# fp32 local attention: clamp on GpSimd, q's length in the score pass instead of the exponentials, squares first in each bank, another order of the steps

## What is computed

```python
h = shift_token(x)
q, k, v = jnp.split(h @ wqkv, 3, axis=-1)       # 128 -> 3 x 512
q = l2norm(q) * qs
k = l2norm(k) * ksc
q, k = rotary_xpos(q, k)                        # q * cos * scale + rotate_half(q) * sin * scale
...
sim = jnp.einsum('bhwid,bhwjd->bhwij', bq, bk)  # q times 8
sim = jnp.where(mask, -jnp.finfo(sim.dtype).max, sim)
attn = jax.nn.softmax(sim, axis=-1)
out = jnp.einsum('bhwij,bhwjd->bhwid', attn, bv)
x = x + out @ wo
```

## Time and profile before

| | us |
|---|---|
| three timed runs | 495.89, 494.99, 490.20 |
| their median | 494.99 |
| the profiled execution | 490.59 |
| its span in the trace | 488.8 |

### The profile page before, as it was taken

The page is one execution under the profiler, slowest core; times in us unless marked ns, Lnnn a source line. Parts: engine busy times, 40 slices in busy tenths (PEclk is TensorE's granted clock), DMA queues, the critical chain, the costliest instruction groups (busy, mean ns, idle before and its releaser), DMA issues.

```text
span 488.8 us, 8090 instructions
## 1 busy us (share of the span) xinstructions
PE 403.8 (83%) x2504; PEld 261.2 (53%) x2504; DVE 366.4 (75%) x1404; ACT 322.5 (66%) x986; POOL 199.5 (41%) x197
## 2 busy tenths in 40 slices
PE   0688858889989998978689678998999899877895
PEld 0466644556655665666434236665666566654342
DVE  2688647999999999985134688999999999750345
ACT  2345532888888888877432267888888888773324
POOL 5260114466556655661100145645664565430000
PEclk9977886999999999989989988999999999897898
DMA  8900000000000000000000000000000000000002
GB/s 172 295 1 1 1 1 0 1 3 1 2 0 2 2 0 2 1 1 2 0 1 0 0 1 2 1 0 3 0 3 1 2 2 0 2 1 1 0 0 86
DMA packets 10264, 7.26 MB, mean 15 GB/s; under 512 B 3245, under 2 KB 9431, under 8 KB 10222
## 3 DMA queue, kind: packets, MB, share of 16 engines
q1 hardware_dynamic: 8590, 5.63, 4.1%
q0 software_dynamic: 832, 1.12, 1.1%
q10 hardware_dynamic: 800, 0.00, 0.1%
HBM read 5.70 MB, written 1.05 MB: 14 GB/s over the span
## 4 chain that ended last, share of the span: by engine, by line
ACT 33%; PE 30%; DVE 29%; issue 5%; DMA 1%; POOL 1%; SPq 0%; POOLq 0%; DVEq 0%; ACTq 0%
ACT pp L760 24%; PE ps L506 9%; DVE ssc L981 5%; PE ps L616 4%; DVE shared L970 4%; DVE kT L1005 4%; ACT sqr L670 4%; ACT oT L769 3%; DVE ss L977 3%; DVE vv L1009 3%; PE ps L379 3%; PE ps L541 2%; PE ps L554 2%; PE ps L530 2%; DVE pri L1001 1%
## 5 line engine op out<-in xcount | busy, mean ns | idle before, releaser
L760 ACT ACTIVATE pp<-pp,nb,rr 128x128 f32<-128x128 f32 x256 | 122.7, 481 | 1.2 <-DVE nb L996 1.2
L340 POOL TENSOR_TENSOR pp<-pp,pri 128x512 f32<-128x512 f32 x64 | 66.5, 1040 | 131.6 <-DVE pri L1001 131.6
L379 PE MATMUL ps<-wqkv_raw,xs 128*128 128x512 f32 x192 | 104.6, 633 | 7.8 <-ACT sqr L670 6.2
L347 POOL TENSOR_TENSOR shared<-shared 128x512 f32<-128x512 f32 x64 | 80.1, 1272 | 66.3 <-DVE shared L970 66.3
L670 ACT ACTIVATE sqr<-ps 128x512 f32<-128x512 f32 x64 | 38.2, 599 | 43.9 <-DVE shared L970 27.8
L987 DVE CUSTOM_DVE_ANT_0 pp<-ps,msk 128x128 f32<-128x128 f32 x256 | 58.6, 283 | 5.7 <-issue 5.7
L506 PE MATMUL ps<-hn,w1g 128*128 128x512 f32 (+1 forms) x96 | 49.2, 634 | 5.8 <-DVE uu L1075 5.8
L760 ACT ACTIVATION_READ_ACCUMULATOR pp<-pp,nb,rr 128x1 f32 x256 | 48.1, 188 | 0.0
L970 DVE TENSOR_TENSOR shared<-ps,stab 128x256 f32<-128x256 f32 x128 | 47.4, 410 | 0.0
L541 PE MATMUL ps<-idn,pp 128*128 128x128 f32 x256 | 38.5, 295 | 10.7 <-DVE kT L1005 10.1
L967 DVE TENSOR_TENSOR shared<-ps,ctab 128x512 f32<-128x512 f32 x64 | 43.5, 679 | 3.2 <-ACT sqr L670 2.9
(11 more groups left out here) (119 smaller groups left out, 682.1 us busy)
## 6 DMA issues: line engine op xcount, KB each, us to landing
wqkv_raw<-in_L_ffn_wqkv_dram SPq DMA_DIRECT2D x1, 1536.0 KB, 14.4
out_dram<-shared SPq DMA_DIRECT2D x4, 256.0 KB, 2.5
w_raw<-in_L_ffn_w_dram SPq DMA_DIRECT2D x1, 682.0 KB
xt<-in_x_dram SPq DMA_DIRECT2D x2, 256.0 KB, 4.3
xt<-in_x_dram SPq DMA_DIRECT2D x1, 512.0 KB, 11.0
wo_raw<-in_L_ffn_wo_dram SPq DMA_DIRECT2D x1, 512.0 KB
ct<-in_ctx_dram POOLq DMA_DIRECT2D x1, 360.0 KB, 9.8
w_raw<-in_L_ffn_w_dram SPq DMA_DIRECT2D x2, 128.0 KB
```

The source lines that it names most:

```text
L340: T(pp[m.j][:, a, :, :], pp[m.j][:, a, :, :], pri[m.j][:, a * 4:a * 4 + 4].unsqueeze(2).to_broadcast([128, PAIRS, 128]), ALU.mult).then_in ...
L347: T(cs[m.j][:, part], cs[m.j][:, part], sn[m.j][:, part], ALU.add).then_inc((aq_done, ak_done)[s], 1)
L379: mm(ps[:, part, :], xs[:, m.b, 0:N], wqkv_raw[:, m.layer, part * INNER:(part + 1) * INNER], start=True, stop=True).then_inc((q_ps, k_ps, ...
L760: A(pp[m.j][:, a, c, :], pp[m.j][:, a, c, :], ACT.Exp, bias=nb[m.j][:, a * 4 + c:a * 4 + c + 1], scale=rr[m.j][:, h:h + 1], accum_out=psum ...
```

## The change

- POOL: `clamped` moves from DVE to POOL, at the end of its step, ahead of k's `rotate`, which is now done one step earlier relative to q's.
- DVE: the passes (`maxima_`) get rr of the head as their scale (a 128x1 operand), add a mask of 0 and +1e30 and keep a minimum instead of a maximum; the tables of q carry a factor -8 instead of 8, so scores arrive negated. The minimum (`nm`) is then the bias of the exponentials as it stands, and `shifts` is gone. The passes now wait for `r_ready`.
- ACT: the exponentials take scale -1.0 and bias nm; there is no 128x1 scale any more.
- ACT and DVE: `squares` reads each bank first (waits for the projection alone) and `turns` follows (waits for the squares); k's `turns` also waits for the transposes of two batches before (its buffer).
- PE: `project_q` waits only for `turns`; `project_k` is now the first reader of a batch's input, one step ahead of `project_q`, and only `project_k` of batch 0 is issued ahead of the pipeline. `project_v` moves one step earlier.
- All: another order inside `step`, and pipelines that begin one step earlier (PE, ACT, DVE at -4 instead of -3, POOL at -3 instead of -2).

```diff
-NEG = -1e30
+FAR = 1e30
...
-    cq, sq = cos * sc * 8.0, sin * sc * 8.0 * sgn
+    cq, sq = cos * sc * -8.0, sin * sc * -8.0 * sgn
...
+            def clamped(m):
+
+                pool.wait_ge(sq_sum, 2 * m.i + 2)
+                nc.gpsimd.tensor_scalar(ssc[m.j][:], ss[m.j][:], 1e-24, None, ALU.max).then_inc(ss_ready, 1)
+
             def step(at, on):
                 if on(0):
-                    normalise(at(0), 0)
+                    normalise(at(0), 1)
                 if on(2):
                     rotate(at(2), 0)
-                    rotate(at(2), 1)
                     unit_k(at(2))
                 if on(1):
-                    normalise(at(1), 1)
+                    normalise(at(1), 0)
+                if on(3):
+                    clamped(at(3))
+                    rotate(at(3), 1)
...
             def project_q(m):
-                if m.b % GB == 0 and m.layer == 0:
-                    pe.wait_ge(x_out, 2 * (m.b // GB) + 2)
-                elif m.b % GB == 0:
-                    pe.wait_ge(f_upd, 2 * ((m.layer - 1) * NG + m.b // GB) + 4)
                 if m.b > 0:
                     pe.wait_ge(tq_done, m.i)
-                    pe.wait_ge(sqq_done, m.i)
                 qkv(m, 0)
...
             def last_group(g):
                 probs_T(g)
                 pe.wait_ge(ld_wqkv, 16)
-                project_q(Batch(0, 0))
                 project_k(Batch(0, 0))
...
             def squares(m, s):
 
-                if s == 0:
-                    act.wait_ge(tq_done, m.i + 1)
-                else:
-                    act.wait_ge(k_ps, m.i + 1)
+                act.wait_ge((q_ps, k_ps)[s], m.i + 1)
...
             def weights(m, a):
 
-                act.wait_ge(nb_ready[a], m.i + 1)
+                act.wait_ge(nm_done[a], m.i + 1)
                 for c in range(PAIRS):
-                    h = 2 * c + a
-                    A(pp[m.j][:, a, c, :], pp[m.j][:, a, c, :], ACT.Exp, bias=nb[m.j][:, a * 4 + c:a * 4 + c + 1],
-                      scale=rr[m.j][:, h:h + 1], accum_out=psum_[m.j][:, a * 4 + c:a * 4 + c + 1]).then_inc(p_done[a], 1)
+                    A(pp[m.j][:, a, c, :], pp[m.j][:, a, c, :], ACT.Exp, bias=nm[m.j][:, a * 4 + c:a * 4 + c + 1],
+                      scale=-1.0, accum_out=psum_[m.j][:, a * 4 + c:a * 4 + c + 1]).then_inc(p_done[a], 1)
...
             def turns(m, s):
 
-                dve.wait_ge((q_ps, sqk_done)[s], m.i + 1)
+                dve.wait_ge((sqq_done, sqk_done)[s], m.i + 1)
+                if s == 1 and m.i >= 2:
+                    dve.wait_ge(kT_ps, m.i - 1)
...
-            def clamped(m):
-                dve.wait_ge(sq_sum, 2 * m.i + 2)
-                V.tensor_scalar(ssc[m.j][:], ss[m.j][:], 1e-24, None, ALU.max).then_inc(ss_ready, 1)
-
             def maxima_(m, a):
 
+                dve.wait_ge(r_ready, m.i + 1)
                 apart(V, s_ps, m.i + 1, a)
                 for c in range(PAIRS):
+                    h = 2 * c + a
                     last = V.tensor_tensor_reduce(out=pp[m.j][:, a, c, :], in0=ps[:, SA + a, c * 128:(c + 1) * 128], in1=msk[:],
-                                                  scale=1.0, scalar=-3e38, op0=ALU.add, op1=ALU.max,
-                                                  accum_out=mx[m.j][:, a * 4 + c:a * 4 + c + 1])
-                last.then_inc(mx_done[a], 1)
-
-            def shifts(m, a):
-
-                dve.wait_ge(mx_done[a], m.i + 1)
-                dve.wait_ge(r_ready, m.i + 1)
-                V.scalar_tensor_tensor(out=nb[m.j][:, a * 4:a * 4 + 4], in0=mx[m.j][:, a * 4:a * 4 + 4], scalar=-1.0,
-                                       in1=rr[m.j][:, a:HEADS:2], op0=ALU.mult, op1=ALU.mult).then_inc(nb_ready[a], 1)
+                                                  scale=rr[m.j][:, h:h + 1], scalar=3e38, op0=ALU.add, op1=ALU.min,
+                                                  accum_out=nm[m.j][:, a * 4 + c:a * 4 + c + 1])
+                last.then_inc(nm_done[a], 1)
```

More of the change, by code:

```diff
@@ L65, in tables @@
     j = np.arange(N)[None, :]
-    mask = np.where((j <= i) & (j >= i - W), 0.0, NEG).astype(np.float32)
+    mask = np.where((j <= i) & (j >= i - W), 0.0, FAR).astype(np.float32)
     return rot, mask, np.eye(128, dtype=np.float32)
@@ L162, in build @@
         zo = pp[1][:, 0, :, :]
-        mx, nb, psum_, pri = (sb2(n, [128, HEADS]) for n in ("mx", "nb", "psum_", "pri"))
+        nm, psum_, pri = (sb2(n, [128, HEADS]) for n in ("nm", "psum_", "pri"))
         pT = [sb(f"pT{k}", [128, 2, PAIRS, 128]) for k in range(2)]
@@ L524, in scores_ @@
                 if m.b > 0:
[L525 to L526 removed]
+                    pe.wait_ge(nm_done[0], m.i)
+                    pe.wait_ge(nm_done[1], m.i)
                 for c in range(PAIRS):
@@ L582, in step @@
                     project_q(at(4))
-                if on(0) and not on(3):
+                if on(0) and at(0).b == B - 3:
                     m = at(0)
[L586 to L593, removed]
+                    pe.wait_ge(layer_w1, m.layer + 1)
+                    pe.wait_ge(tk_done, m.end)
+                    pe.wait_ge(tq_done, m.end)
+                    hidden(m.layer, 0, 0)
+                if on(0) and not on(1):
+                    hidden(at(0).layer, 0, 1)
                 if on(0):
                     deviation(at(0))
-                if on(4):
-                    project_k(at(4))
+                if on(1):
+                    weights_T(at(1), 0)
                 if on(0) and not on(1):
@@ L629, in _ @@
             for layer in range(DEPTH):
-                pipeline(pe, layer, step, -3, before={-3: lambda: out_T(NG - 1)} if layer == 0 else {})
+                pipeline(pe, layer, step, -4, before={-3: lambda: out_T(NG - 1)} if layer == 0 else {})
                 hidden(layer, 0, 2, [1])
@@ L785, in step @@
             def step(at, on):
[L786 to L791, removed]
+                if on(1):
+                    weights(at(1), 0)
                 if on(0):
@@ L795, in step @@
                     weights(at(1), 1)
-                    weights(at(1), 0)
+                if on(2):
+                    q_rows(at(2))
+                if on(4):
+                    squares(at(4), 1)
                 if on(0):
                     dev_square(at(0))
-                if on(2):
-                    q_rows(at(2))
+                if on(3):
+                    lengths(at(3))
                 if on(0):
@@ L803, in step @@
                 if on(1):
+                    weights_out(at(1), 0)
+                if on(4):
+                    squares(at(4), 0)
+                if on(1):
                     weights_out(at(1), 1)
-                    weights_out(at(1), 0)
             def unshifted(g):
@@ L818, in _ @@
             for layer in range(DEPTH):
-                pipeline(act, layer, step, -3, before={-3: lambda: results(NG - 1)} if layer == 0 else {})
+                pipeline(act, layer, step, -4, before={-3: lambda: results(NG - 1)} if layer == 0 else {})
                 nc.scalar.preload_act_table_set("gelu_and_others")
@@ L1026, in step @@
             def step(at, on):
+                if on(1):
+                    maxima_(at(1), 0)
+                    maxima_(at(1), 1)
                 if on(3):
-                    turns(at(3), 0)
-                if on(1):
-                    m = at(1)
-                    for a in (1, 0):
-                        maxima_(m, a)
-                        shifts(m, a)
-                if on(3):
-                    turns(at(3), 1)
+                    squared(at(3), 0)
+                    squared(at(3), 1)
                 elif on(2):
@@ L1066, in _ @@
             for layer in range(DEPTH):
-                pipeline(dve, layer, step, -3)
+                pipeline(dve, layer, step, -4)
                 def gate(gl_, c):
```

42 lines of the change are left out of this document (20 added, 22 removed).

## The result

| | before | after |
|---|---|---|
| timed runs, us | 495.89, 494.99, 490.20, 491.04 | 454.29, 451.75, 449.06, 453.69 |
| median | 493.01 | 452.72 |
| profiled execution / its span | 490.59 / 488.8 | 454.29 / 452.5 |
| step of the attention pipeline | 9.65 | 8.32 |

The ratio of the times is 0.917 (95% interval 0.909 to 0.926): about 40 us faster. The forecast was 462 us, range 450 to 479.

A forecast was written before the change was run, and what follows sets the result against it. No engine alone bound the kernel: ACT and DVE made each other wait; PE (8.56 us) would be next. Step 9.67 to 8.6, times 28, 30 us off 490.6 gives 460.6, placed at 462 us, range 450 to 479.

The forecast's parts named there:

- The step and the sum: Attention pipeline: step falls from 9.67 to 8.6 us, times 28 steps, 30 us off.
- case 1: PE becomes the bound of the attention step: 70%, own range 450 to 470 us.
- PE's own work, 8.56 us: PE in an attention step: 9.67 us less 1.11 of waiting leaves 8.56, the most work of any engine.
- DVE's own work, 8.41 us: DVE in an attention step: 9.28 - 1.03 - 0.33 + 0.49 = 8.41 us after the change.
- a rival at 17%: DVE becomes the bound of the attention step at 9.0 to 9.2 us, total 472 to 478: 17%.
- The operand: 128x1 scale moved: each pass on DVE 0.06 us longer, each exponential on ACT 0.085 us shorter.
- The clamp: Moved from DVE to POOL: frees 1.03 us of DVE per step, takes 0.3 us on POOL, hidden.
- The shifts: Two DVE operations of 0.16 us per step go, 0.33 us of DVE, and a wait of the exponentials.
- Squares first, costed at nothing: ACT's squares ahead of DVE's turns: takes ACT's 0.98 us wait out of the chain; late squares costed at nothing.
- The order, costed at nothing: New order in the step: each batch's loops fit, the longest 7.4 us, below 8.6; no cost.
- The ends, nothing: Layer starts and ends: an extra nearly empty step and later q, against 1.4 us a layer off exponentials: nothing.
- Rivals 3 and 4: Longest loop takes over, 485 to 492 us: 8%; passes with two SBUF operands shut out by POOL, 504 us: 5%.

The follow-up runs named there:

- b5_clamp_scale: Kernel before with the clamp on POOL and the scale in the passes (no shifts), old order, q's squares behind its turn: step 8.21 us, one execution 444.4 us.
- b1_clamp: Kernel before with only the clamp moved to POOL, old order: step 9.43 us against 9.65, one execution 483.7 us.

## Why the prediction was right, point by point

- **The step and the sum.** Predicted 8.6 us and 30 us; measured 8.39 in the mean and 36. Time and range held, the step was mis-sized by 0.2, which is 6 of the 9 us between 462 and 453. The rest is 1.4 us that the forecast was placed above its own sum, and the scatter of the runs. The time lies near the lower end of the range, which case 1 had reached with a step of 8.35 by one more reading of PE's starts.
- **PE's own work, 8.56 us.** This term failed by 0.24. The list in the new order is 8.32 (immediate scale: PE's rows have no gap), and in the old order, to which the 8.56 belonged, it is at most 8.21 (`b5_clamp_scale`), so there the term was at least 0.35 too high. I had taken off 0.24 us before `attend`, which is the drained idle time only. By starts `attend` began 1.40 us after the scores in the earlier trace rows, and 1.10 (142.19 - 141.09) is what the scores take with nothing to wait for: 0.30. The projection ahead of the deviation occupies 0.86 us (147.39 to 148.25) and not the 0.97 that I took from one ahead of transposes, so its wait was 0.53 and not 0.42. The deviation occupies 0.22 us instead of the 0.33 that I read off; why it is longer there was not tested.
- **DVE's own work, 8.41 us.** 8.32 measured in the new order, and at most 8.21 in the old one, from which the 8.41 was taken: too high for the same reason as PE's term, since I subtracted drained idle time and durations. By the starts in the kernel before, DVE's wait for the last exponential is 1.07 - 0.60 = 0.47 us and not 0.39 (the 0.60 is the same pair in the fence of `b5_clamp_scale`), and the clamp occupies 1.65 - 0.59 = 1.06 us and not 1.03:

```profile
156.01 0.69 DVE L977 TENSOR_REDUCE ss<-sqr 128x8 f32<-128x512 f32 x1
157.08 0.18 DVE L1001 RECIPROCAL pri<-psum 128x4 f32<-128x4 f32 x1 [0.39 <-ACT pp L760]
...
157.90 0.68 DVE L977 TENSOR_REDUCE ss<-sqr 128x8 f32<-128x512 f32 x1
...
159.55 0.68 DVE L1009 COPY vv<-ps 128x512 f32<-128x512 f32 x1
```

I had DVE second to PE and called it a rival at 17%. In fact both are full: taking work off either one alone does not shorten the step. The forecast that PE becomes the bound is half right.

- **The operand.** A pass costs 0.064 us more (0.347 against 0.283), predicted 0.06; an exponential 0.092 less (0.389 against 0.481), predicted 0.085. The Trainium skill's 0.093 us for such an operand (ScalarE: Activation LUTs, What ACT_TABLE_LOAD costs) is the better figure.
- **The clamp.** On POOL 0.246 us, predicted 0.3, and hidden. That it was held by POOL's rotation is shown. But that moving it frees 1.03 us of DVE was wrong for the clamp by itself: in the old order the shut-out passes to the first shift, and 0.22 us is left. The shifts were costed at 0.16 each and were the other half of the pair. That the terms add up in the change as a whole is luck in part: the prediction did not see the hand-over, and the shifts happen to be gone too.
- **Squares first, costed at nothing.** The whole came out as forecast, and in the new order no row of PE waits, but the price of squares first by itself was measured in the old order only. There it costs 0.93 us alone (9.65 to 10.58) and 1.98 beside clamp and scale. My reason that it takes the 0.98 us of ACT's wait out of the chain is refuted: moving the clamp takes that wait away with the squares still behind the turn (`b1_clamp`, `b5_clamp_scale`), and the scale alone leaves it at 0.98. The wait came from the clamp ahead of the turn on DVE.
- **The order, costed at nothing.** With q's squares first it is worth 1.87 us, 10.19 to 8.32, more than the whole gain. Order and squares first together lose 0.11 us beside clamp and scale (8.21 to 8.32) and gain 0.95 without them (9.65 to 8.70). The prediction saw that in the new order q's squares stand well ahead of its turn, and that held. It did not see that they cost 2 us without that order, nor that the two together gain on the kernel before, so that both could be put at nothing is luck in part.
- **The ends, nothing.** 36.3 - 36.0 = 0.3 us, in part by luck: 0.9 us went before the second batch's scores of layer 1 and 1.4 between the layers, while the part behind the last scores grew by 2.0 us, at a lower granted clock than before (0.83 against 0.88, last section).
- **Rivals 3 and 4.** No loop took over, and passes with two operands from SBUF were not shut out (0.347 us mean over 256).

## What to carry to other kernels

A small VectorE operation that lasts as long as a GpSimd instruction beside it is being shut out; look for the next candidate before it is moved, since taking one away may only hand the wait to another. Do the parts of a change one at a time in both orders: here two parts were worth 0.6 us apart and 1.44 together, and a third part was harmful without the order that came with it. Take work off each of two engines alone and off both: if neither alone helps, the third run tells two full engines from some other bound. Read an engine's own work from places where it runs without waiting, not as a step less the idle time that its rows name.

## What was not expected of the hardware

POOL shut out a DVE operation with two inputs in SBUF of only 128x4 elements (1.01 us instead of 0.16), not only the clamp. The Trainium skill (SBUF — State Buffer, Who interferes with whom) says so of DVE instructions with two SBUF inputs beside a GpSimd instruction that reads SBUF; this trace agrees, with k's multiplication as that instruction. The passes, with one tensor in PSUM, a mask and a 128x1 operand in SBUF, are not held.

The granted clock of the feed-forward part of layer 2 differs from one execution to another, and its time with it. After the last scores of layer 2 the changed kernel and its variant with an immediate scale do nearly the same work (first row the changed kernel, second the variant; us, then busy times and instructions of PE, PEld, DVE, ACT and POOL, granted clock, DMA):

```profile
393.30:452.50 59.20, 46.80 (x169) 25.32 (x168) 22.15 (x51) 23.12 (x51) 2.08 (x2) 0.83 0.06 18
```

```profile
391.80:444.40 52.60, 40.23 (x169) 20.80 (x168) 21.67 (x51) 23.05 (x51) 2.08 (x2) 0.99 0.07 20
```

The same 169 matmul records take 6.6 us longer at a granted clock of 0.83 than at 0.99. In the full steps in the middle of the layers it is 1.00 in every kernel. This is why the variant's 446.2 us against 454.3 says nothing on the passes: its steps are the same. The same stretch of the kernel before and of `b5_clamp_scale`:

```profile
431.62:488.80 57.18, 44.92 (x167) 23.38 (x166) 22.42 (x54) 22.93 (x49) 2.08 (x2) 0.88 0.07 19
```

```profile
390.42:442.40 51.98, 40.54 (x167) 20.78 (x166) 22.70 (x52) 22.26 (x49) 2.08 (x2) 0.99 0.07 20
```

So 7.2 of the 9.9 us between `b5_clamp_scale` and the changed kernel lie here. How much of the scatter between executions of one kernel comes from this clock is not shown, since each kernel has one trace. Why the clock falls in one execution and not in another stays open.
